# First attention's mapped keys: one float32 product replaced by two rounded products on stacked high and low parts, with the prologue that this needs and ten first score products issued twice

## What is computed

```python
c_q  = h_t @ W_DQ + b_DQ            # 32 latent channels
c_kv = h_t @ W_DKV + b_DKV          # 32
q_c = c_q @ W_UQ + b_UQ             # 8 heads x 128
k_c = c_kv @ W_UK + b_UK
v_c = c_kv @ W_UV + b_UV
q_r = c_q @ W_QR + b_QR             # 8 heads x 32
k_r = h_t @ W_KR + b_KR             # 32, the same for all heads
scores = concat(q_c, q_r) . concat(k_c, k_r) * scale
attn = softmax(scores)
return (attn @ v_c) @ W_O + b_O
```

## Time and profile before

| | |
|---|---|
| median of 3 runs | 842.99 us (839.82 to 844.04) |
| profiled execution, its own time | 842.36 us |
| its span, first to last instruction | 840.5 us |
| mean granted TensorE clock | 0.984 of 2.4 GHz |
| busy share of the span | PE 92%, DVE 73%, ACT 60%, POOL 49% |
| prologue, until unit 0's first score | 59.4 us |
| first attention's units | 59.4 to about 336 us |
| first unit of the second attention | about 501 to 553 us |

### The profile page before, as it was taken

One profiled execution on the slowest core, in us unless ns is written; L12 is line 12 of the kernel. 1 busy time (PEld: TensorE's weight loads), 2 busy tenths in 40 slices (PEclk: granted clock), 3 DMA queues, 4 the chain that ended last, 5 costly groups with the idle time before them and its releaser, 6 DMA issues.

```text
span 840.5 us, 13859 instructions
## 1 busy us (share of the span) xinstructions
PE 770.1 (92%) x4602; PEld 451.0 (54%) x4602; DVE 613.3 (73%) x1611; ACT 505.5 (60%) x864; POOL 408.9 (49%) x466
## 2 busy tenths in 40 slices
PE   5899999999999998989999988699999999999986
PEld 2454444444444433579888864355555555554554
DVE  6877687786877798865237668687778777787555
ACT  3335665757656576346546445467777777776772
POOL 3506866667757583707060686967344132220121
PEclk9879999999999999999999999999999999999999
DMA  9400000000000000123131020000000000000001
GB/s 345 175 0 1 1 1 1 1 1 1 1 1 1 2 1 1 48 70 113 61 92 58 26 89 26 20 6 1 1 2 2 1 2 1 1 1 1 2 1 51
DMA packets 14539, 25.35 MB, mean 30 GB/s; under 512 B 3174, under 2 KB 9192, under 8 KB 14344
## 3 DMA queue, kind: packets, MB, share of 16 engines
q1 hardware_dynamic: 11798, 18.85, 6.4%
q0 software_dynamic: 2048, 4.20, 1.6%
q10 hardware_dynamic: 626, 1.43, 0.5%
HBM read 15.03 MB, written 9.44 MB: 29 GB/s over the span
## 4 chain that ended last, share of the span: by engine, by line
PE 36%; DVE 14%; POOL 6%; issue 4%; ACT 2%; DMA 0%; ACTq 0%; POOLq 0%; DVEq 0%
PE ps L1677 6%; PE ps L1762 6%; PE ps L1742 4%; DVE ps L2534 3%; PE ps L1648 3%; DVE mx_part L2537 3%; PE ps L1630 2%; PE ps L1640 2%; PE ps L1631 2%; PE ps L1632 2%; POOL xnT L659 1%; PE ps L1595 1%; PE ps L1770 1%; PE ps L1831 1%; PE ps L1543 1%
## 5 line engine op out<-in xcount | busy, mean ns | idle before, releaser
L2053 DVE TENSOR_REDUCE mx_part<-ps 128x1 f32<-128x512 f32 x256 | 163.8, 682 | 59.1 <-PE ps L1322 58.3
L1114 ACT ACTIVATE pt<-ps 128x1024 f32<-128x1024 f32 (+1 forms) x160 | 149.7, 938 | 69.5 <-PE ps L1742 68.0
L907 ACT ACTIVATE pt<-ps 128x512 f32<-128x512 f32 x256 | 140.9, 596 | 70.4 <-PE ps L1347 64.0
L1677 PE MATMUL ps<-rounded 128*128 128x128 f32 (+2 forms) x352 | 123.6, 384 | 12.1 <-DVE mx_part L2534 4.5
L2534 DVE CUSTOM_DVE_ANT_0 ps<-ps,wm 128x128 f32<-128x128 f32 (+3 forms) x256 | 119.6, 518 | 18.8 <-PE ps L1677 17.7
L859 ACT ACTIVATE rounded<-ps 128x512 fp32r<-128x512 f32 (+3 forms) x160 | 94.3, 591 | 63.8 <-PE ps L1311 22.3
L1347 PE MATMUL ps<-rounded 100*128 100x512 f32 x256 | 120.8, 484 | 10.6 <-ACT pt L907 9.7
L722 POOL TENSOR_SCALAR_AFFINE_SELECT pt<-pt 128x512 f32<-128x512 f32 x64 | 39.9, 636 | 167.7 <-ACT pt L1114 167.6
L1742 PE MATMUL ps<-rounded 128*128 128x512 f32 (+2 forms) x352 | 115.5, 368 | 0.7 <-ACT rounded L859 0.7
L1322 PE MATMUL ps<-rounded 98*128 98x512 f32 x256 | 105.7, 431 | 2.2 <-DVE mx_part L2053 1.2
L2537 DVE TENSOR_REDUCE mx_part<-ps 128x1 f32<-128x512 f32 x128 | 82.4, 686 | 31.0 <-PE ps L1677 30.8
(11 more groups left out here) (308 smaller groups left out, 1288.6 us busy)
## 6 DMA issues: line engine op xcount, KB each, us to landing
wm<-in_wm SPq DMA_DIRECT2D x1, 4896.0 KB, 16.1
to_experts<-kstage SPq DMA_DIRECT2D x6, 512.0 KB, 4.6
of_experts<-pt SPq DMA_DIRECT2D x12, 256.0 KB, 2.0
kstage<-to_experts SPq DMA_DIRECT2D x10, 256.0 KB, 2.7
wm<-in_experts SPq DMA_DIRECT2D x1, 1540.0 KB, 7.6
x<-in_x SPq DMA_DIRECT2D x4, 256.0 KB, 5.9
out<-x SPq DMA_DIRECT2D x4, 256.0 KB, 2.3
early<-in_wo ACTq DMA_DIRECT2D x1, 512.0 KB
```

Of the source, the lines that this page charges most:

```text
L907: nc.scalar.activation(pt0(k, i), ps[:, ST0_BANKS[i % 2], :], ACT.Exp, scale=SCALE0).then_inc(exp_done, 1)
L1114: nc.scalar.activation(pt[:, 4 * (t % 2) + 2 * g:4 * (t % 2) + 2 * g + 2, 0:w], ps[:, ST1_BANKS[2 * g]:ST1_BANKS[2 * g] + 2, 0:w], ACT.Exp ...
L1677: ins = mm(bank[:, o:o + w], queries1(u, i), keys[:, 0:w], start=(o == 0), stop=(o == parts[-1][1]))
L2053: v.tensor_reduce(mx_part[u % 2][:, o:o + 1], ps[:, max_bank(u, n), :], AX_X, ALU.max).then_inc(max_done, 1)
```

## The change

The keys' 64 rows are now made twice, in one product of 128 columns: ACT rounds all 128 rows into `kvr` (now the tiles `qstage`), and DVE writes the low part over the second 64. The map is split in the same way into `zmap_hi` and `zmap_lo`, each doubled along the partitions, in the tile `first_stack`. A mapped-key product is now two float32r products of 128 rows that accumulate. The row of ones is gone: the bias that it carried is a column `zbias`, which ACT adds in its copy and DVE in its low part. The prologue makes the doubled maps on PE (one more product of one column a head, for the bias), ACT, DVE and POOL. The keys' transposes become products with `both`. Ten of unit 0's maximum pieces are issued twice into the same bank. In the second attention POOL loses a memset of 4096 columns (to ACT, in two halves) and the layernorm's last step of quarter 2 (to DVE); its mask of step 4 is moved before the staging of keys, and one memset of `qstage` is moved to where POOL waits for expert slots.

```diff
+TWICE_AT = (5, 7, 9, 11, 15, 17, 19, 21, 29, 31)
-VALUE_MAPS_AT, VALUE_BIAS_AT = {22: (0, 0), 24: (0, 1), 25: (1, 0), 27: (1, 1)}, {28: 0, 30: 1}
+VALUE_MAPS_AT, VALUE_BIAS_AT = {23: (0, 0), 25: (0, 1), 27: (1, 0), 29: (1, 1)}, {30: 0, 31: 1}
+LATENT_ROWS, ROTARY_ROWS = [[slice(r, r + DC) for r in (r0, r0 + 2 * DC)] for r0 in (0, DC)]
...
+            for n, rows in enumerate(ROTARY_ROWS):
+                pool.wait_ge(qr_hi, n + 1)
+                nc.gpsimd.tensor_tensor(zmap_lo[rows], qr_rows[rows], zmap_hi[rows].bitcast(F32),
+                                        ALU.subtract).then_inc(qr_lo, 1)
+            pool.wait_ge(qr_lo, len(ROTARY_ROWS))
...
-            pool.wait_ge(m1_split, 2)
-            nc.gpsimd.memset(key_stack1[1].rearrange("p r n -> p (r n)").bitcast(F32), 0.0).then_inc(keys_zero[1], 1)
             gather(2, range(2))
...
-                if k == 3:
+                if k == 4:
                     stage_keys(2, 0)
-                if k >= 3:
-                    gather(3, [k - 3])
-                if k == 5:
-                    second_xn(2)
+                if k >= 4:
+                    gather(3, [k - 4])
             stage_queries(2, 0)
+            gather(3, [3])
...
-                copy(zmap[0:DC, 4 * g:4 * g + 4, :], v[0:DC]).then_inc(prep_done, 1)
-                copy(zmap[64:65, 4 * g:4 * g + 4, :], v[64:65]).then_inc(prep_done, 1)
+                copy(zbias[:, 4 * g:4 * g + 4], ps[0:NZ, PREP_BANKS[g], 4 * NZ:4 * NZ + 4])
+                for rows in LATENT_ROWS:
+                    ins = copy(zmap_hi[rows, 4 * g:4 * g + 4, :], v[rows])
+                ins.then_inc(prep_done, 2)
             act.wait_ge(proj_in, 16 * PROJ_LOADS)
             first_xnT(0)
-            first_cq(0)
+            act.wait_ge(qr_in, 16 * len(ROTARY_ROWS))
+            for rows in ROTARY_ROWS:
+                copy(zmap_hi[rows], qr_rows[rows]).then_inc(qr_hi, 1)
...
+            def z_products(u, k, h, c):
+                o, keys = ps[0:NZ, z_bank(u, k), :], kvr[u // UH][:, c * CH:(c + 1) * CH]
+                mm(o, zmap_lo[:, h, :], keys, start=True, stop=False)
+                return mm(o, zmap_hi[:, h, :], keys, start=False, stop=True)
...
-                mm(ps[0:NZ, z_bank(u, k), :], zmap[:, h0 + h, :], kvr[:, b * S + c * CH:b * S + (c + 1) * CH],
-                   start=True, stop=True).then_inc(z_mm, 1)
+                z_products(u, k, h0 + h, c).then_inc(z_mm, 1)
...
+                for _ in range(2 if u == 0 and n in TWICE_AT else 1):
+                    ins = mm(ps[:, max_bank(u, n), :], cq[0:NZ, b * S + j * P:b * S + (j + 1) * P],
+                             key_stack[u % 2][0:NZ, h, c * CH:(c + 1) * CH], start=True, stop=True)
+                ins.then_inc(s_mm, 1)
...
-                v.tensor_tensor(key_stack[pp][rows, h, cols], ps[rows, z_bank(u, k), :],
-                                key_stack[pp][rows, h, cols].bitcast(F32), ALU.subtract).then_inc(z_lo, 1)
+                v.scalar_tensor_tensor(out=key_stack[pp][rows, h, cols], in0=ps[rows, z_bank(u, k), :],
+                                       scalar=zbias[rows, n:n + 1], in1=key_stack[pp][rows, h, cols].bitcast(F32),
+                                       op0=ALU.add, op1=ALU.subtract).then_inc(z_lo, 1)
+
+            def first_kv_lo(c):
+                lo = kvr[c // QH][64:P, c % QH * CH:(c % QH + 1) * CH]
+                dve.wait_ge(kv_hi, c + 1)
+                v.scalar_tensor_tensor(out=lo, in0=ps[64:P, KV_BANKS[c], :], scalar=bkv[64:P, 0:1],
+                                       in1=lo.bitcast(F32), op0=ALU.add, op1=ALU.subtract).then_inc(kv_lo, 1)
...
+                if c == QH and n == N_NORM - 1:
+                    dve.wait_ge(norm_step, (c + 1) * N_NORM)
+                    dve.wait_ge(norm_turn, c)
+                    for t in range(TC):
+                        v.tensor_scalar(xn[:, t, :], x[:, c * TC + t, :], mv[:, t, 0:1], norm[:, 0, 3, t:t + 1],
+                                        ALU.subtract, ALU.mult).then_inc(norm_xn, 1)
```

More of the change, by code:

```diff
@@ L332, in build @@
         qstage = [sb(f"qstage{i}", [P, TS, HG, RS], F32R) for i in range(2)]
+        kvr = [q[:].rearrange("p t h w -> p (t h w)") for q in qstage]
         blocks = kstage[1][:].bitcast(F32).rearrange("p t h w -> p (t h w)").rearrange("p (q k n) -> p q k n", q=2, k=QUAD)
@@ L575, in _ @@
             nc.gpsimd.memset(kstage[0][:].bitcast(F32), 0.0).then_inc(consts, 1)
-            nc.gpsimd.memset(qstage[0][:].bitcast(F32), 0.0).then_inc(consts, 1)
             for hf in range(QH):
@@ L665, in _ @@
             scatter(0)
+            pool.wait_ge(z_mm, 4 * U0)
+            nc.gpsimd.memset(qstage[0][:].bitcast(F32), 0.0).then_inc(queries_zero, 1)
             nc.gpsimd.memset(first_stack[:, 0:HG, :].bitcast(F32), 0.0).then_inc(first_zero, 1)
@@ L885, in first_kv @@
                 act.wait_ge(kv_mm, c + 1)
-                nc.scalar.activation(kvr[0:DC + DR, c * CH:(c + 1) * CH], ps[0:DC + DR, KV_BANKS[c], :], ACT.Identity,
-                                     bias=bkv[:, 0:1]).then_inc(kv_done, 1)
+                nc.scalar.activation(kvr[c // QH][:, c % QH * CH:(c % QH + 1) * CH], ps[:, KV_BANKS[c], :], ACT.Identity,
+                                     bias=bkv[:, 0:1]).then_inc(kv_hi, 1)
             def first_ckv(b):
@@ L897, in z_hi_copy @@
                 act.wait_ge(z_mm, u * 4 + (k + 1))
-                copy(key_stack[pp][0:NZ, h, c * CH:(c + 1) * CH], ps[0:NZ, z_bank(u, k), :]).then_inc(z_hi, 1)
+                n = u % UH * HP + h
+                nc.scalar.activation(key_stack[pp][0:NZ, h, c * CH:(c + 1) * CH], ps[0:NZ, z_bank(u, k), :], ACT.Identity,
+                                     bias=zbias[:, n:n + 1]).then_inc(z_hi, 1)
             def exp0(u, pp, k, i):
@@ L2173, in _ @@
                 norm_chunk(c)
+            zmap_low(0)
+            zmap_low(1)
             half_stats(0, 2)
             dve.wait_ge(proj_in, 16 * PROJ_LOADS)
+            v.tensor_tensor(both[:], ident[:, 0:DC], ident[:, 2 * DC:3 * DC], ALU.add).then_inc(both_ok, 1)
+            first_kv_lo(0)
             first_cq_lo(0)
@@ L2721, in lay_out @@
         "x": a["L0_attn_h_t"].reshape(T, D),
[L2722 removed]
+        "uk": np.concatenate([np.concatenate([uk[:, h0:h0 + 2].reshape(DK, 2 * DC)] * 2, 1) for h0 in range(0, H0, 2)]
+                             + [ukb[:, :, 0]], 1),
         "uq": np.concatenate([uq, uq, uq, ubq, ubq], 2),
```

144 lines of the change are left out of this document (89 added, 55 removed).

## The result

The changed kernel takes 838.96 us, median of 7 executions (837.87 to 843.04), against 842.99 of the kernel before, now over 7 executions too (839.82 to 844.04). The ratio is 0.9958, 95% interval 0.9939 to 0.9977. I had forecast 829 and a range of 822 to 836.

The account below looks back on a forecast made before the run. PE was taken to set the pace in the units, with small stalls. Units -9.0, prologue -0.5 and second attention -4.3 sum to -13.8 from 842.4: 828.6, forecast 829, range 822 to 836 for 8 in 10.

Parts of the forecast that it names:

- Mapped-key products: In the units, a key product becomes two rounded products, 0.47 us instead of 0.86: 0.39 saved each, 26 times, 10.1 us.
- Units, -9.0: First attention's units: 10.1 us saved, less 1.1 for ACT's bias copies; DVE's low part hidden; bounds -10.1 and none.
- the first rival: Units: the saving turns into PE's waits for ACT's exponentials; 833.5 us with half the gain, 838 with none; chance 0.15.
- Prologue's start: Prologue: the first key product waits for POOL's rotary low parts until 18.0; DVE's first maximum moves from 19.70 to 21.4.
- Prologue's length: Prologue: DVE's chain 28.0 us without waits, before 25.6; with the start, -0.5 in all, ends -3.5 and +4.2.
- The doubled pieces: Prologue: ten maximum pieces cost PE 0.235 us each at full clock, mostly where it waited for DVE; may hold the clock.
- the chain that ends at 53.5: Prologue: DVE's chain to its last maximum if the clock holds part of the time, 3 to 5 us of waits staying.
- the slower rival: Prologue: half clock from the first score to unit 0, +19.3 us there, about 849 in all; chance 0.05.
- the prologue gets longer: Prologue: clock low as before, POOL's low parts delay the start, waits stay; +4.2 instead of -0.5, 833.5; chance 0.12.
- my sign of being wrong: Wrong if the seven-unit stretch stays above 247 us and exponential waits grow, or unit 0 starts after 62 us.
- Second attention, -4.3: Second attention's first unit: PE's waits for POOL, 2.96 and 1.88 us, go; DVE gets 1.1 to 2.3 work; bounds -2, -6.
- the first two rivals together: Units and prologue: the saving turns into waits and the prologue is longer as well, giving no change; chance 0.05.

Follow-up runs that it names:

- e6_z_twice: The changed kernel with the 26 mapped-key products of the units issued twice: 849.74 us, ratio 1.0090 to the kernel before.
- e7_recip: The changed kernel with DVE's fourth reciprocal of each unit written ahead of the maxima of step 2: 838.17 us, ratio 0.9963 to the kernel before.
- e3_turns: The changed kernel with the keys' turns in one float32r instruction each instead of two: 841.10 us, ratio 0.9987 to the kernel before.
- the kernel with three edits: The changed kernel with one-instruction turns, the fourth reciprocal ahead, and the rotary weights' high copies in ACT's gap: 885.14 us against 887.24 before, ratio 0.9967.
- the first eight kernels: The follow-up kernels run on two chips on which the kernel before took 842.5 and 841.5 us.
- the last four: The follow-up kernels run where the kernel before took 887.2 us at a clock of 0.960; the changed kernel itself did not run beside them.
- e1_same: The changed kernel run and profiled again, no edit: 840.32 us, ratio 0.9986 to the kernel before.
- e10_qr_gap: The changed kernel with ACT's high copies of the rotary weights moved between its two groups of map copies: 891.20 us against 887.24 before, ratio 1.0046.
- e5_second_only: The kernel before with only the second attention's part of the change: 840.53 us, ratio 0.9989 to the kernel before.
- e8_both: The changed kernel with one-instruction keys' turns and the fourth reciprocal ahead of the maxima: 883.46 us against 887.24 before, ratio 0.9956.

## Why the prediction was wrong

**Mapped-key products.** Right: 0.39 us saved each, at full clock, 26 times.

**Units, -9.0; measured -6.9.** The mechanism was the first rival's, saving turned into waits, but at another engine: I charged ACT's copies with a bias 1.1 us, and PE's waits for exponentials did not move. I put DVE at nothing, "it is busy 195 of 250 us, and hides it". That is the step that failed: an average over the stretch says nothing of the one place where DVE's last reciprocal was already what PE waited for (0.5 us in three waits, in the same view of before). The low parts themselves grew little, from 0.70 to 0.76 us each; it is mostly the saved time that ends in that wait. e6_z_twice and e7_recip show it from both sides: with the reciprocal ahead the units are 9.3 us shorter than before, of the 10.1 that I had counted at most. Of the rest I know only that ACT's waits for POOL's sums grew from 3.2 to 4.3 us; no run took this apart.

**Prologue's start, 21.4 for DVE's first maximum; measured 21.89 and 22.10.** It came 0.5 and 0.7 later than forecast, and the reason holds only in part. POOL's low parts ended at 18.05, as forecast (18.0), with the first key product right behind them, and I called the move from 19.70 theirs. But with the clock's rise at 16.5 us the old prologue, which has no such parts, has its first key product at 17.99 and its first maximum at 21.87. The profile of before had caught an early rise, so its 59.4 was a favourable start of the account. That the number was nearly right is in good part luck.

**Prologue's length, from DVE's first maximum to unit 0's first score: 2.2 shorter by the forecast (58.9 - 21.4 against 59.4 - 19.7); measured 4.5 longer at equal half clock.** This is the step that failed and cost the forecast. I built the sum from DVE's chain and the waits of before, and counted what was added on DVE, but not what was added on PE. The keys' turns were in the diff as one clause and in my sum not at all: twice the instructions, each twice as long (0.213 us from start to start at half clock instead of 0.107), 5.4 us more of PE (3.46 + 1.92 + 1.75 against 1.06 + 0.68), mostly at half clock where DVE waits for PE. e3_turns gives 2.3 to 2.6 us of the prologue back. The doubled pieces I took as nearly free, and hoped that they would hold the clock. It did not hold: 17.1 to 23.9 us of half clock in the profiles of the unchanged new prologue (10.2 in one), against 17.1 and 13.7. They cost 2.0 in one pair of profiles and 0 to 1.2 in the other. Whether they hold the clock at all stays open: without them one prologue had 23.9 us, as one with them had, and in the kernel with three edits both had 20.5. Two sums have slips: the chain that ends at 53.5 is 1.1 early, and I took 1.4; and the slower rival's 48 - 33.2 + 4.7 is 19.5, not 19.3. The rival "the prologue gets longer" at +4.2 was nearest, though the first score came later still (+6.7 and +8.7, and my sign of being wrong, a start of unit 0 after 62 us, was there); I had given it 0.12.

**Second attention, -4.3; measured -1.6 to -2.2 at equal half clock, -1.0 and -2.4 by the medians.** The waits for POOL went as forecast. I named DVE as what is late next, and then credited its idle time against its new work. Its idle time lay before a norm that now runs into it: from 533.95 to 545.95 us it pauses for more than 0.1 us only twice, 0.41 us in all; three of its small steps take 0.6 instead of 0.16 while POOL works beside it; and PE waits for its maxima. The measured value is at my bound of -2, not at the one taken.

**The clock.** I had not charged it. The profile of before says 0.984 and its 64 executions beside the first eight kernels average 0.984; the changed kernel averages 0.980 over 12 executions, and 0.982 over its first seven. By the executions of all kernels outside the last four, each kernel with a level of its own, 0.01 goes with 4.7 us; by those of the kernel before alone, with 3.4. So my estimate is that some 1 to 1.6 us of the forecast gain went there in e1_same; they are part of the terms above.

The sum of the measured terms, +6.7 - 6.9 - 2.1 = -2.3, stands at the near end of the -2.2 and -4.0 of the two sets of medians. The time of 839 to 840 is thus the first two rivals together, part of the saving turned into waits and a longer prologue, to which I had given 0.05.

## What to carry to other kernels

When an edit makes one kind of product cheaper by splitting its operands, list every other product that reads these operands: here the keys' turns doubled in number and in price and ate about a third of what the cheap products gave (2.3 to 2.6 us of 6.9). Before a saving on the pacing engine is summed, look for the first wait behind each place where it is made; one that exists already, however short, takes the saving, and it may be cured by the order of one instruction on the other engine. And compare prologues at equal granted clock, with more than one profile: here one profile of each kernel differed by 8.7 us at the first score, of which about 4 were clock, and a gain of 2 us in the second attention came out only when profiles with equal half clock were set side by side.

## What the runs showed of the hardware

- A POOL `TENSOR_TENSOR` of 784 columns and a DVE `TENSOR_SCALAR` on 128 columns, both from SBUF, did not share time but excluded each other: in e10_qr_gap two single DVE steps of 0.34 us became 1.91 and 1.98, and each ended within 0.1 us of one of POOL's two operations (1.97 and 1.83). The Trainium skill, Trainium Architecture — The Big Picture (What this means for kernel authors), calls the port that DVE and GpSimd share "an exclusive lock (not a bandwidth split)"; the trace agrees, step by step. DVE operations that read PSUM (0.76 us for a low part), and its statistics (0.26 to 0.29), were not slowed beside the same POOL work in e1_same.
- The program does not start at full clock. The record of the granted clock begins, at full, at 11.3 us in one execution and at 15.8 to 22.8 in the other thirteen profiled (a window ahead of that prints 1.00, for want of a record). Ahead of it the two instructions of a float32 product of 512 columns stand twice as far apart: up to 0.99 us in e5_second_only, 0.48 to 0.52 in the profile of before behind its rise.
- The clock fell while PE was at work: in e1_same at 50.6 us, behind 13.65 us of full clock in which PE was busy 89% of the time and never idle for more than 0.31 us; in the kernel before at 42.1, behind 10.24 us with 83% and at most 1.3 us.
- A keys' turn is a product of 32 columns from 128 rows; its instructions stand 0.213 us apart at half clock and 0.112 at full, in float32 as in float32r (e1_same and e8_both). Only the number of instructions differs, two against one. The turn of before, a transpose of 32 rows in one instruction, had 0.107 at half clock and 0.062 at full.
